# A mixture of experts whose first layer goes from split fp32r products to fp32 products on quarter tiles of TensorE

## The chip, the cores and the metric

The kernel runs on one NeuronCore of a Trainium2 chip. The metric is the time of one execution in microseconds (us), lower is better. The kernel before takes 583.3 us (median of three runs, 582.72 to 583.43).

## The reference, cut to what matters

There are 16 steps of 784 tokens, each token a vector of D = 64. Every step is embedded, runs through one step of a recurrent cell, and then through a mixture of 16 experts, of which the two with the highest logits count. The part that the change touches is the gate and the expert layers:

```python
gate_logits = x @ gate_w + gate_b                 # x: tokens x 64, gate_w: 64 x 16
topk_vals, topk_idx = jax.lax.top_k(gate_logits, 2)
topk_w = softmax(topk_vals)
h = relu(einsum('bsh,ehf->bsef', x, w1) + b1)     # w1: 16 x 64 x 128, first layer
expert_out = einsum('bsef,efh->bseh', h, w2) + b2 # w2: 16 x 128 x 64, second layer
y = x + sum(topk_w * selected expert_out)         # then a layer norm
```

The input x of this part is a layer norm of the cell's output (here x2). The recurrence makes a step wait for the one before it.

## The kernel before

All 16 experts are computed for all tokens, and the gates, zero for 14 of 16, weight the results. A step's tokens are 7 tiles of 112; in transposed form they are 784 columns, worked in two halves of 392 (HALF). Four stages of different steps run beside each other in one body of a software pipeline: embedding (step t+3), cell and norm (`mix`, t+2), gate (t+1), experts (t), and closing norm (t-1). The body goes through 16 units u, and every engine has its own in-order list of work placed at units; there is no planner. Bodies 0 to 12 hold nearly everything, bodies 13 to 15 less and less.

- **x2.** VectorE writes x2 (L481), ScalarE a copy of it rounded to fp32r (L459, `hi`), VectorE the remainder (L598, `lo`). The two stand beside each other, so one TensorE transpose per tile (`x2_turn`, L675, at u = 1) puts hi in partitions 0 to 63 and lo in 64 to 127. ScalarE copies that to xt (L384, L385, `keep_xt`).
- **Logits** (L686, u = 3): per tile one fp32r product over 128 rows, against gate weights that are split in the same way, with 32 output columns; VectorE adds the two parts and the bias (L487, L490).
- **First layer** (`first_layer`, L711), once for each expert: for each half of the columns two fp32r products with 128x128 weights (w1hi, then w1lo) into the same bank. Expert e uses pZ[e % 2] (two banks, one for each half) and waits for the ReLU of expert e-2.
- **ReLU** (L426, ScalarE), once for each expert over all 784 columns, pZ to hexp.
- **Second layer** (L724, `second_layer`, at odd u, one pair of experts late): per half two fp32 products with 128x64 weights, one on either half of the array's columns, into pO.
- **Product and sum** (VectorE L543 and L559): pO + bias, times the gates that are spread over the partitions, added up; the first sum of a step starts from xt.

ScalarE's other work stands between the ReLUs, at these units: 1 keep_xt, 2 keep_xn1t (L407, L408), 3 new_hidden (L413, L415), 5 keep_h1 (L377), 6 exp (L442), 7 a square, 8 close_center and a square (L393, L389), 9 a square, 10 the gates' copy (L447), 12 the copy of x2 (L459), 14 close_norm (L398, seven small ones). TensorE's: 1 x2_turn, 2 embed_turn (L645, waits for xt), 3 logits and recur (L653, L654, wait for keep_xn1t), 5 hidden_turn (L660) and embed_in (L635, waits for the load of xcur), 7 sum_turn (L735), 10 gates_turn (L695).

Before the first body ScalarE rounds all of w1 (L439) and GpSimd computes the remainder (L354).

Of the kernel before, what the change touches and what calls it, by code (L numbers as in the profile page):

```python
# [5 lines left out]
def vit_tower_kernel(nc, x_in, tok_w, tok_b, w_ih, w_hh, b_ih, b_hh, gate_w, gate_b,  # L6
# [18 lines left out]
    f32r = mybir.dt.float32r  # L25
# [5 lines left out]
    D = w_ih.shape[0]  # L31
# [25 lines left out]
    with ctx:  # L57
# [15 lines left out]
        w1f = sb("w1f", [2 * D, E, F])  # L73
        w1hi = sb("w1hi", [2 * D, E, F], f32r)
        w1lo = sb("w1lo", [2 * D, E, F], f32r)
        gwf = sb("gwf", [2 * D, E])
        gwhl = sb("gwhl", [2 * D, 2 * E], f32r)
# [26 lines left out]
        x2 = sb("x2", [P, TILES, D])  # L104
        x2hl = sb("x2hl", [P, TILES, 2, D], f32r)
        xt = [sb(f"xt{i}", [2 * D, TOK], f32r) for i in range(2)]
# [34 lines left out]
        MIX = Chain("mix_stage", "pre hid_odd hid hid_turned h2 square var rstd x2 hi lo "  # L141
                                 "turned_a turned_b xt_a xt_b")
        GATE = Chain("gate_stage", "logits hi_part biased max1 hit1 ranked1 first1 best1 without "
# [14 lines left out]
        gw_split = sem("gate_w_split")  # L158
        w1_split = sem("w1_split")
# [52 lines left out]
        for k in range(2):  # L212
            rows = slice(k * D, (k + 1) * D)
            cell_loads += [(cell[rows, k, :], w_ih), (cell[rows, 1 - k, :], w_hh),
                           (rbias[rows, 0:1], b_ih.unsqueeze(1)), (rbias[rows, 1:2], b_hh.unsqueeze(1)),
                           (gwf[rows, :], gate_w)]
            expert_loads += [(w1f[rows, :, :], w1)]
        cell_loads += [(gbias[:, :], gate_b.partition_broadcast(P))]
# [81 lines left out]
        def _(pool):  # L300
# [48 lines left out]
            def body(t, par, experts=False, gate=False, mix=False, embed=False, close=False):  # L349
                if close:  # L350
                    add_beta(t - 1)
                if known(t, 0) and gate:
                    pool.wait_ge(w1_split, 1)
# [18 lines left out]
        def _(act):  # L372
# [44 lines left out]

            def body(t, par, experts=False, gate=False, mix=False, embed=False, close=False):
                for u in range(E):
                    if experts:  # L420
                        n = t * E + u
                        act.wait_ge(z_ready, n + 1)
                        if not known(n, RING):

                            act.wait_ge(y_ready, t * E + 2 * (u // 2) - RING + 2)
# [11 lines left out]
                    if known(t, 0) and gate and u == 4:  # L437
                        act.wait_ge(experts_loaded, EXPERTS_LOADED)
# [26 lines left out]
            act.wait_ge(cell_loaded, CELL_LOADED)  # L465
            nc.scalar.activation(gwhl[:, 0:E], gwf[:, :], ACT.Copy).then_inc(gw_split, 1)
# [7 lines left out]
        def _(dve):  # L474
# [9 lines left out]
            def bias_logits(s):  # L484
                GATE.wait(dve, s, "logits")
                parts = pB[0:P, 0:TILES * 2 * E].rearrange("p (i k e) -> p k i e", e=E, k=2)
                nc.vector.tensor_tensor(lg[:, :, :], parts[:, 0, :, :], over_tiles(gbias[:, :], E), ALU.add)\  # L487
                    .then_inc(GATE.sem, 1)
                GATE.wait(dve, s, "hi_part")
                nc.vector.tensor_tensor(lg[:, :, :], parts[:, 1, :, :], lg[:, :, :], ALU.add).then_inc(GATE.sem, 1)  # L490
# [57 lines left out]
            def add(step, q, par):  # L548

                n = step * Q + q  # L550
                dve.wait_ge(p_ready, 2 * n + 2)
                if q == 0:

                    MIX.wait(dve, step, "xt_b")
                    sofar = xt[par][:, :].bitcast(f32)
                else:
                    dve.wait_ge(summed, n)
                    sofar = acc[par][:, :]
                nc.vector.tensor_tensor(acc[par][:, :], sofar, prod[q % RING][:, :], ALU.add).then_inc(summed, 1)  # L559

            def body(t, par, experts=False, gate=False, mix=False, embed=False, close=False):
                g, s, a, c = t + 1, t + 2, t + 3, t - 1
                for u in range(E):
# [30 lines left out]
                    if mix and u == 12:  # L594
                        norm_scale(MIX, s, 1, x2[:, :, :], h2[:, :, 0:D])
                    if mix and u == 14:
                        MIX.wait(dve, s, "hi")
                        nc.vector.tensor_tensor(x2hl[:, :, 1, :], x2[:, :, :], x2hl[:, :, 0, :].bitcast(f32),  # L598
                                                ALU.subtract).then_inc(MIX.sem, 1)
# [5 lines left out]
            dve.wait_ge(gw_split, 1)  # L605
            nc.vector.tensor_tensor(gwhl[:, E:2 * E], gwf[:, :], gwhl[:, 0:E].bitcast(f32), ALU.subtract)\
                .then_inc(gw_split, 1)
# [11 lines left out]
        def _(pe):  # L619
# [45 lines left out]
            def x2_turn(s):  # L665

                MIX.wait(pe, s, "lo")
# [5 lines left out]
                for bank, first, end in ((pA, 0, PAIRS), (pB, PAIRS, TILES)):  # L673
                    for i in range(first, end):
                        last = nc.tensor.transpose(bank[:, (i - first) * P:(i - first + 1) * P],  # L675
                                                   x2hl[:, i, :, :].bitcast(f32).rearrange("p a d -> p (a d)"),
# [3 lines left out]
            def logits(s, par):  # L680

                MIX.wait(pe, s, "xt_b")
                if known(s, 1):
                    pe.wait_ge(gw_split, 2)
# [15 lines left out]
            def first_layer(t, e, par):  # L700

                n = t * E + e
                if e == 0:
                    MIX.wait(pe, t, "xt_b")
                if known(n, 1):
                    pe.wait_ge(w1_split, 2)
                if not known(n, 2):
                    pe.wait_ge(h_ready, n - 1)
                for b in range(2):
                    for k, w in enumerate((w1hi, w1lo)):  # L710
                        last = nc.tensor.matmul(halves(pZ[e % 2])[:, b, :], w[:, e, :],  # L711
                                                xt[par][:, b * HALF:(b + 1) * HALF], start=(k == 0), stop=(k == 1))
                last.then_inc(z_ready, 1)

            def second_layer(t, q):

                n = t * Q + q
                pe.wait_ge(h_ready, 2 * n + 2)
                for b in range(2):
                    if not known(n, 1):  # L720
# [84 lines left out]
```

## Time and profile before

| | |
|---|---|
| runs | 583.43, 583.3, 582.72 us |
| the profiled execution | 584.91 us, its span 583.1 us |
| mean granted TensorE clock | 0.985 |
| TensorE busy | 534.7 us (92%) |
| VectorE busy | 430.0 us (74%) |
| ScalarE busy | 356.2 us (61%) |
| GpSimd busy | 170.2 us (29%) |
| chain that ended last | TensorE 78%: pZ L711 29%, pO L724 28% |

Busy times are sums over one profiled execution. A TensorE record is longer than the distance to the next one, since records overlap; what an instruction costs is read from start to start. The "chain that ended last" follows the execution back from its end, each time to what released the instruction.

### The profile page before, as it was taken

To read this page: it belongs to the slowest core of one execution; us is meant where nothing else is said; L and a number is where in the kernel's file an instruction comes from. 1 tells how busy PE (TensorE), PEld (TensorE's weight loads), DVE (VectorE), ACT (ScalarE), POOL (GpSimd) and SP (SyncE) were. 2 spreads that over 40 slices of the span, in tenths; PEclk is the share of its full clock that TensorE was granted. 3 is DMA by queue.
4 is the path that set the end of the run, shared out by engine and by line. 5 is a ranking of instruction groups with operands and counts; after the bars stand their busy time and mean duration, and the time that the engine had idled before them with its cause. 6 is when DMAs were issued, how large, how long until landed. Compare 5 with 4: busy or idle time off the path is not lost.

```text
span 583.1 us, 8948 instructions
## 1 busy us (share of the span) xinstructions
PE 534.7 (92%) x3138; PEld 358.0 (61%) x3138; DVE 430.0 (74%) x819; ACT 356.2 (61%) x596; POOL 170.2 (29%) x133
## 2 busy tenths in 40 slices
PE   2577999999999999999999999999999999999991
PEld 2365666576666767576666767576666657565640
DVE  1144868978787878978787888878787797886762
ACT  2236665767567674757667675757667475846561
POOL 4122011513132241513242241523232151311334
PEclk9999999999999999999999999999999899998996
DMA  3304683563819184562909174562809265462801
GB/s 79 95 15 107 146 191 75 137 145 74 194 31 233 32 181 101 125 156 63 203 22 229 46 177 105 121 161 65 203 18 219 60 142 125 107 146 71 184 0 42
DMA packets 30140, 67.45 MB, mean 116 GB/s; under 512 B 7056, under 2 KB 12432, under 8 KB 29968
## 3 DMA queue, kind: packets, MB, share of 16 engines
q1 hardware_dynamic: 30096, 66.89, 49.4%
q8 instruction: 25, 0.41, 0.3%
q14 instruction: 19, 0.16, 0.1%
HBM read 59.59 MB, written 7.28 MB: 115 GB/s over the span
## 4 chain that ended last, share of the span: by engine, by line
PE 78%; DVE 5%; ACT 5%; DMA 4%; issue 4%; POOL 2%; SPq 1%; POOLq 0%; DVEq 0%; ACTq 0%
PE pZ L711 29%; PE pO L724 28%; PE pA L660 4%; PE pA L735 4%; PE pB L635 4%; DMA xcur<-x_in 4%; ACT hexp L426 2%; PE pA L653 2%; PE pB L686 2%; PE pA L645 2%; PE pA L675 1%; DVE acc L559 1%; POOL inv_std L327 1%; SPq L293 1%; PE pB L695 1%
## 5 line engine op out<-in xcount | busy, mean ns | idle before, releaser
L426 ACT ACTIVATE hexp<-pZ,b1c 128x784 f32<-128x784 f32 x256 | 229.5, 908 | 83.1 <-PE pZ L711 80.9
L543 DVE SCALAR_TENSOR_TENSOR prod<-pO,b2c,spread 128x392 f32<-128x392 f32 x256 | 151.6, 623 | 98.4 <-PE pO L724 91.8
L724 PE MATMUL pO<-hexp,w2s 128*64 128x392 f32 x1024 | 199.8, 506 | 1.3 <-ACT hexp L426 1.3
L711 PE MATMUL pZ<-xt,w1hi 128*128 128x392 f32 x512 | 194.8, 380 | 3.7 <-ACT hexp L426 2.3
L711 PE MATMUL pZ<-xt,w1lo 128*128 128x392 f32 x512 | 175.7, 343 | 0.0
L711 PEld LDWEIGHTS pZ<-xt,w1hi 128*128 128x128 f32 x512 | 97.5, 190 | 64.1 <-issue 36.2
L327 POOL TENSOR_TENSOR inv_std<-var,nhalf 112x7 f32<-112x7 f32 x48 | 74.7, 1566 | 174.5 <-DVE var L477 174.5
L724 PEld LDWEIGHTS pO<-hexp,w2s 128*64 128x64 f32 x1024 | 70.4, 137 | 79.2 <-issue 63.9
L559 DVE TENSOR_TENSOR acc<-acc,prod 128x784 f32<-128x784 f32 x112 | 118.4, 1057 | 0.1
L711 PEld LDWEIGHTS pZ<-xt,w1lo 128*128 128x128 f32 x512 | 97.9, 191 | 0.0
L334 POOL TENSOR_TENSOR h2b<-h2c,bet 112x448 f32<-112x448 f32 x16 | 20.2, 1263 | 169.0 <-DMA h2c<-h_dram 169.0
L377 ACT ACTIVATE h<-pB 112x455 f32<-112x455 f32 x16 | 8.8, 551 | 56.2 <-PE pB L635 56.2
L477 DVE TENSOR_REDUCE var<-sq 112x7 f32<-112x455 f32 x48 | 28.6, 622 | 12.9 <-ACT sq L389 12.9
L660 PEld LDWEIGHTS pA<-half_fold,state 128*112 128x112 f32 x224 | 25.7, 193 | 13.2 <-issue 8.6
L342 POOL TENSOR_TENSOR yn<-yn,gam 112x448 f32<-112x448 f32 x16 | 18.5, 1153 | 52.1 <-ACT yn L398 52.1
L735 PEld LDWEIGHTS pA<-fold,acc 128*112 128x112 f32 x224 | 23.2, 178 | 12.6 <-issue 8.6
L660 PE MATMUL pA<-half_fold,state 128*112 128x65 f32 x224 | 28.0, 282 | 3.0 <-ACT state L415 3.0
L398 ACT ACTIVATE yn<-cen,inv_std 112x64 f32<-112x64 f32 x112 | 28.3, 336 | 2.3 <-POOL inv_std L327 2.3
L635 PE MATMUL pB<-tokw,xcur 65*112 65x65 f32 x224 | 28.7, 287 | 1.0 <-DMA xcur<-x_in 0.6
L635 PEld LDWEIGHTS pB<-tokw,xcur 65*112 65x112 f32 x224 | 27.0, 202 | 2.9 <-issue 1.4
L735 PE MATMUL pA<-fold,acc 128*112 128x64 f32 x224 | 25.4, 265 | 2.7 <-DVE acc L559 2.7
L347 POOL TENSOR_TENSOR yo<-yn,h2b 112x448 f32<-112x448 f32 x16 | 27.4, 1713 | 1.3
(74 smaller groups left out, 425.6 us busy)
## 6 DMA issues: line engine op xcount, KB each, us to landing
spread<-gates_dram SPq DMA_DIRECT2D x128, 392.0 KB, 9.0
h_dram<-h SPq DMA_DIRECT2D x16, 199.1 KB, 2.5
h2c<-h_dram SPq DMA_DIRECT2D x16, 199.1 KB, 9.7
xcur<-x_in SPq DMA_DIRECT2D x16, 196.0 KB, 9.9
out<-yo SPq DMA_DIRECT2D x16, 196.0 KB, 9.3
w1f<-w SPq DMA_DIRECT2D x2, 512.0 KB, 6.1
w2s<-w SPq DMA_DIRECT2D x1, 512.0 KB, 6.8
gates_dram<-gt SPq DMA_DIRECT2D x16, 28.0 KB, 2.0
```

Source lines behind the costliest of these rows:

```text
L327: nc.gpsimd.tensor_tensor(inv_std[:, lane, :], var[:, lane, :], nhalf[:, :], ALU.pow)\
L347: nc.gpsimd.tensor_tensor(yo[:, :, :], yn[:, :, :], h2b[:, :, :], ALU.add).then_inc(CLOSE.sem, 1)
L398: last = nc.scalar.activation(yn[:, i, :], cen[:, i, :], ACT.Copy, scale=inv_std[:, 2, i:i + 1])
L426: nc.scalar.activation(hexp[u % RING][:, :].rearrange("p (b c) -> p b c", b=2), halves(pZ[u % 2]), ACT.Relu, bias=b1c[:, u:u + 1])\
L477: nc.vector.tensor_reduce(var[:, lane, :], sq[:, lane, :, :], X, ALU.add).then_inc(chain.sem, 1)
L543: nc.vector.scalar_tensor_tensor(out=prod[q % RING][:, b * HALF:(b + 1) * HALF], in0=halves(pO)[:, b, :], scalar=b2c[:, q:q + 1], in1=spre ...
L559: nc.vector.tensor_tensor(acc[par][:, :], sofar, prod[q % RING][:, :], ALU.add).then_inc(summed, 1)
L635: last = nc.tensor.matmul(tiles_and_mean(pB)[:, i, :], xcur[:, i * P:(i + 1) * P], tokw[:, :], start=True, stop=True)
L660: last = nc.tensor.matmul(tiles_and_mean(pA)[:, i, :], state[:, i % 2, (i // 2) * P:(i // 2 + 1) * P], half_fold[:, i % 2, :], start=True, ...
L711: last = nc.tensor.matmul(halves(pZ[e % 2])[:, b, :], w[:, e, :], xt[par][:, b * HALF:(b + 1) * HALF], start=(k == 0), stop=(k == 1))
L724: last = nc.tensor.matmul(halves(pO)[k * D:(k + 1) * D, b, :], w2s[:, e, :], hexp[e % RING][:, b * HALF:(b + 1) * HALF], start=True, stop= ...
L735: last = nc.tensor.matmul(tiles_of(pA)[:, i, :], acc[par][:, i * P:(i + 1) * P], fold[:, 0:D], start=True, stop=True)
```

## The change

w1 is no longer split. It is held once, even experts in partitions 0 to 63 and odd ones in 64 to 127. x2 is written in fp32 (L481) and copied once (ScalarE, `twice`), so that after the transpose xt holds x2 in both halves of the partitions. The first layer works on a pair of experts at a time, at even u: for each half of the columns four fp32 products with 64x64 weights, for two experts (rows) and two halves of their 128 outputs (columns). Its semaphore rises once for each half, and the ReLUs come as two instructions of 392 columns, one for each expert, for one half at each unit u. The logits are fp32 products over 64 rows with 16 output columns. The first sum starts from 0.5 * xt.

```diff
-                nc.vector.tensor_tensor(lg[:, :, :], parts[:, 0, :, :], over_tiles(gbias[:, :], E), ALU.add)
-                GATE.wait(dve, s, "hi_part")
-                nc.vector.tensor_tensor(lg[:, :, :], parts[:, 1, :, :], lg[:, :, :], ALU.add).then_inc(GATE.sem, 1)
+                nc.vector.tensor_tensor(lg[:, :, :], fresh, over_tiles(gbias[:, :], E), ALU.add).then_inc(GATE.sem, 1)
...
+            def relu_half(t, q, b):
+                n = t * Q + q
+                act.wait_ge(z_ready, 2 * n + b + 1)
+                if not known(n, 2):
+                    act.wait_ge(y_ready, 2 * (n - 2) + b + 1)
+                if known(n, 1) and b == 0:
+                    act.wait_ge(experts_loaded, EXPERTS_LOADED)
+                for e in (2 * q, 2 * q + 1):
+                    nc.scalar.activation(hexp[e % RING][:, b * HALF:(b + 1) * HALF], halves(pZ[e % 2])[:, b, :],
+                                         ACT.Relu, bias=b1c[:, e:e + 1]).then_inc(h_ready, 1)
...
-                        nc.scalar.activation(hexp[u % RING][:, :].rearrange("p (b c) -> p b c", b=2),
-                                             halves(pZ[u % 2]), ACT.Relu, bias=b1c[:, u:u + 1])\
-                            .then_inc(h_ready, 1)
+                        relu_half(t, u // 2, u % 2)
...
-                        nc.scalar.activation(w1hi[:, :, :], w1f[:, :, :], ACT.Copy).then_inc(w1_split, 1)
...
-                    nc.gpsimd.tensor_tensor(w1lo[:, :, :], w1f[:, :, :], w1hi[:, :, :].bitcast(f32), ALU.subtract)\
-                        .then_inc(w1_split, 1)
...
-                        nc.scalar.activation(x2hl[:, :, 0, :], x2[:, :, :], ACT.Copy).then_inc(MIX.sem, 1)
+                        nc.scalar.activation(x2[:, :, 1, :], x2[:, :, 0, :], ACT.Copy).then_inc(MIX.sem, 1)
...
-                        nc.vector.tensor_tensor(x2hl[:, :, 1, :], x2[:, :, :], x2hl[:, :, 0, :].bitcast(f32),
-                                                ALU.subtract).then_inc(MIX.sem, 1)
...
+                    nc.vector.scalar_tensor_tensor(out=acc[par][:, :], in0=xt[par][:, :], scalar=0.5,
+                                                   in1=prod[q % RING][:, :], op0=ALU.mult, op1=ALU.add)\
+                        .then_inc(summed, 1)
...
-                    last = nc.tensor.matmul(pB[0:P, i * 2 * E:(i + 1) * 2 * E], xt[par][:, i * P:(i + 1) * P],
-                                            gwhl[:, :], start=True, stop=True)
+                    last = nc.tensor.matmul(pB[0:P, i * E:(i + 1) * E], xt[par][0:D, i * P:(i + 1) * P], gw[:, :],
+                                            start=True, stop=True)
...
-                if not known(n, 2):
-                    pe.wait_ge(h_ready, n - 1)
                 for b in range(2):
-                    for k, w in enumerate((w1hi, w1lo)):
-                        last = nc.tensor.matmul(halves(pZ[e % 2])[:, b, :], w[:, e, :],
-                                                xt[par][:, b * HALF:(b + 1) * HALF], start=(k == 0), stop=(k == 1))
-                last.then_inc(z_ready, 1)
+                    if not known(n, 1):
+                        pe.wait_ge(h_ready, 4 * (n - 1) + 2 * b + 2)
+                    for k in range(2):
+                        rows = slice(k * D, (k + 1) * D)
+                        for c in range(2):
+                            some = slice(c * D, (c + 1) * D)
+                            last = nc.tensor.matmul(halves(pZ[k])[some, b, :], w1s[rows, q, some],
+                                                    xt[par][rows, b * HALF:(b + 1) * HALF], start=True, stop=True)
+                    last.then_inc(z_ready, 1)
...
-                pe.wait_ge(h_ready, 2 * n + 2)
                 for b in range(2):
+                    pe.wait_ge(h_ready, 4 * n + 2 * b + 2)
...
-                    if experts:
-                        first_layer(t, u, par)
+                    if experts and u % 2 == 0:
+                        first_layer(t, u // 2, par)
```

## Rows read from the trace of the kernel before

**Rows 1.** Fourteen steps: stretch, length, PE, PEld, DVE, ACT, POOL busy, clock.
```profile
51.28:510.86 459.58, 452.38 (x2717) 302.08 (x2717) 368.98 (x709) 305.29 (x509) 134.43 (x92) 1.00 0.55 126
```
**Rows 2.** Groups by line and form: shapes, count | busy us, mean ns | idle before.
```profile
L724 PE MATMUL pO<-hexp,w2s 128*64 128x392 f32 x1024 | 199.8, 506 | 1.3 <-ACT hexp L426 1.3
...
L498 DVE TENSOR_TENSOR hit<-lg,tv 112x112 f32<-112x112 f32 x32 | 12.2, 380 | 1.1
...
L598 DVE TENSOR_TENSOR x2hl<-x,x2hl 112x448 fp32r<-112x448 f32 x16 | 9.9, 621 | 1.3 <-ACT x2hl L459 1.3
...
L490 DVE TENSOR_TENSOR lg<-pB,lg 112x112 f32<-112x112 f32 x16 | 4.4, 274 | 0.5
```
**Rows 3.** Timeline of TensorE, last body: start us, us, line, shapes.
```profile
542.60 0.45 PE L711 MATMUL pZ<-xt,w1hi 128*128 128x392 f32 x1
...
544.21 1.54 PE L724 MATMUL pO<-hexp,w2s 128*64 128x392 f32 x8
545.68 0.45 PE L711 MATMUL pZ<-xt,w1hi 128*128 128x392 f32 x1
```
**Rows 4.** Line 724 on TensorE in the stretch 304.72 to 305.05 us.
```profile
L724 PE MATMUL pO<-hexp,w2s x2: 543/543/543, 304.7 to 304.7; 128*64 128x392 f32 x2
```
**Rows 5.** Timeline of TensorE from expert 14 to expert 1 of the next step.
```profile
306.19 0.45 PE L711 MATMUL pZ<-xt,w1hi 128*128 128x392 f32 x1
...
308.18 1.54 PE L724 MATMUL pO<-hexp,w2s 128*64 128x392 f32 x8
309.64 0.45 PE L711 MATMUL pZ<-xt,w1hi 128*128 128x392 f32 x1
...
311.54 1.54 PE L724 MATMUL pO<-hexp,w2s 128*64 128x392 f32 x8
```
**Rows 6.** Timeline of TensorE from expert 2 to recur.
```profile
314.11 0.34 PE L711 MATMUL pZ<-xt,w1hi 128*128 128x392 f32 x1
314.29 0.34 PE L711 MATMUL pZ<-xt,w1lo 128*128 128x392 f32 x1
314.97 0.57 PE L645 MATMUL pA<-ident,xn 112*128 112x112 f32 x4 [0.34 <-ACT xt L385]
...
316.10 0.77 PE L686 MATMUL pB<-gwhl,xt 128*112 128x32 f32 x7
316.80 0.59 PE L653 MATMUL pA<-state,cell 128*64 128x448 f32 x1
```
**Rows 7.** Timeline of TensorE: hidden_turn, then embed_in.
```profile
322.11 1.59 PE L660 MATMUL pA<-half_fold,state 128*112 128x65 f32 x14
323.54 1.54 PE L635 MATMUL pB<-tokw,xcur 65*112 65x65 f32 x14
```
**Rows 8.** Timeline of ScalarE: close_center and square, copy of x2, close_norm, new_hidden.
```profile
298.36 0.54 ACT L393 ACTIVATE cen<-pA 112x448 f32<-112x448 f32 x1
...
299.41 0.90 ACT L426 ACTIVATE hexp<-pZ,b1c 128x784 f32<-128x784 f32 x1
300.21 0.57 ACT L389 ACTIVATE sq<-h 112x448 f32<-112x448 f32 x1
...
305.83 0.58 ACT L459 ACTIVATE x2hl<-x 112x448 fp32r<-112x448 f32 x1 [0.79 <-DVE x L481]
...
308.02 1.76 ACT L398 ACTIVATE yn<-cen,inv_std 112x64 f32<-112x64 f32 x7
309.69 2.88 ACT L426 ACTIVATE hexp<-pZ,b1c 128x784 f32<-128x784 f32 x3
...
317.82 0.54 ACT L413 ACTIVATE state<-pA,rb 64x336 f32<-64x336 f32 x1 [0.36 <-PE pA L654]
318.38 0.63 ACT L415 ACTIVATE state<-pA,rb 64x448 f32<-64x448 f32 x1
```
**Rows 9.** Timeline of all engines before the first expert: GpSimd's remainder, VectorE beside it.
```profile
39.88 4.51 POOL L354 TENSOR_TENSOR w1lo<-w1f,w1hi 128x2048 fp32r<-128x2048 f32 x1 [10.26 <-ACT w1hi L439]
...
41.67 2.84 DVE L498 TENSOR_TENSOR hit<-lg,tv 112x112 f32<-112x112 f32 x1
```

More of the change, by code:

```diff
@@ L24, in vit_tower_kernel @@
     f32 = mybir.dt.float32
-    f32r = mybir.dt.float32r
     i32 = mybir.dt.int32
@@ L72, in vit_tower_kernel @@
         rb = sb("rb", [2 * D, 1])
[L73 to L77, printed above, removed]
+        w1s = sb("w1s", [2 * D, Q, F])
+        gw = sb("gw", [D, E])
         b1c = sb("b1c", [F, E])
@@ L103, in vit_tower_kernel @@
         h2 = sb("h2", [P, TILES, D + 1])
-        x2 = sb("x2", [P, TILES, D])
-        x2hl = sb("x2hl", [P, TILES, 2, D], f32r)
-        xt = [sb(f"xt{i}", [2 * D, TOK], f32r) for i in range(2)]
+        x2 = sb("x2", [P, TILES, 2, D])
+        xt = [sb(f"xt{i}", [2 * D, TOK]) for i in range(2)]
         lg = sb("lg", [P, TILES, E])
@@ L140, in vit_tower_kernel @@
         EMBED = Chain("embed_stage", "h1 kept square var rstd norm turned xn1t_odd xn1t")
-        MIX = Chain("mix_stage", "pre hid_odd hid hid_turned h2 square var rstd x2 hi lo "
+        MIX = Chain("mix_stage", "pre hid_odd hid hid_turned h2 square var rstd x2 twice "
                                  "turned_a turned_b xt_a xt_b")
-        GATE = Chain("gate_stage", "logits hi_part biased max1 hit1 ranked1 first1 best1 without "
+        GATE = Chain("gate_stage", "logits biased max1 hit1 ranked1 first1 best1 without "
                                    "max2 hit2 ranked2 first2 best2 diff exp den p1 p2 g1 g2 gates turned gt")
@@ L214, in vit_tower_kernel @@
             cell_loads += [(cell[rows, k, :], w_ih), (cell[rows, 1 - k, :], w_hh),
[L215 to L218, printed above, removed]
+                           (rbias[rows, 0:1], b_ih.unsqueeze(1)), (rbias[rows, 1:2], b_hh.unsqueeze(1))]
+            expert_loads += [(w1s[rows, :, :], w1.rearrange("d (q k) f -> k d q f", k=2)[k])]
+        cell_loads += [(gw[:, :], gate_w), (gbias[:, :], gate_b.partition_broadcast(P))]
         expert_loads += [(b1c[:, :], b1), (w2s[:, :, :], w2), (b2c[:, :], b2),
@@ L351, in body @@
                     add_beta(t - 1)
-                if known(t, 0) and gate:
-                    pool.wait_ge(w1_split, 1)
-                    nc.gpsimd.tensor_tensor(w1lo[:, :, :], w1f[:, :, :], w1hi[:, :, :].bitcast(f32), ALU.subtract)\
-                        .then_inc(w1_split, 1)
                 if mix:
@@ L420, in body @@
                     if experts:
[L421 to L425, printed above, removed]
-                        nc.scalar.activation(hexp[u % RING][:, :].rearrange("p (b c) -> p b c", b=2),
-                                             halves(pZ[u % 2]), ACT.Relu, bias=b1c[:, u:u + 1])\
-                            .then_inc(h_ready, 1)
+                        relu_half(t, u // 2, u % 2)
                     if gate and u == 1:
@@ L436, in body @@
                         new_hidden(t + 2)
-                    if known(t, 0) and gate and u == 4:
-                        act.wait_ge(experts_loaded, EXPERTS_LOADED)
-                        nc.scalar.activation(w1hi[:, :, :], w1f[:, :, :], ACT.Copy).then_inc(w1_split, 1)
                     if gate and u == 6:
@@ L594, in body @@
                     if mix and u == 12:
-                        norm_scale(MIX, s, 1, x2[:, :, :], h2[:, :, 0:D])
-                    if mix and u == 14:
-                        MIX.wait(dve, s, "hi")
-                        nc.vector.tensor_tensor(x2hl[:, :, 1, :], x2[:, :, :], x2hl[:, :, 0, :].bitcast(f32),
-                                                ALU.subtract).then_inc(MIX.sem, 1)
+                        norm_scale(MIX, s, 1, x2[:, :, 0, :], h2[:, :, 0:D])
             dve.wait_ge(consts, EPS_SET)
@@ L665, in x2_turn @@
             def x2_turn(s):
-                MIX.wait(pe, s, "lo")
+                MIX.wait(pe, s, "twice")
                 if not known(s, 1):
@@ L675, in x2_turn @@
                         last = nc.tensor.transpose(bank[:, (i - first) * P:(i - first + 1) * P],
-                                                   x2hl[:, i, :, :].bitcast(f32).rearrange("p a d -> p (a d)"),
+                                                   x2[:, i, :, :].rearrange("p a d -> p (a d)"),
                                                    ident[0:P, 0:P])
@@ L698, in gates_turn, with first_layer @@
                 last.then_inc(GATE.sem, 1)
-            def first_layer(t, e, par):
-                n = t * E + e
-                if e == 0:
+            def first_layer(t, q, par):
+                n = t * Q + q
+                if q == 0:
                     MIX.wait(pe, t, "xt_b")
                 if known(n, 1):
-                    pe.wait_ge(w1_split, 2)
-                if not known(n, 2):
-                    pe.wait_ge(h_ready, n - 1)
+                    pe.wait_ge(experts_loaded, EXPERTS_LOADED)
                 for b in range(2):
-                    for k, w in enumerate((w1hi, w1lo)):
-                        last = nc.tensor.matmul(halves(pZ[e % 2])[:, b, :], w[:, e, :],
-                                                xt[par][:, b * HALF:(b + 1) * HALF], start=(k == 0), stop=(k == 1))
-                last.then_inc(z_ready, 1)
+                    if not known(n, 1):
[7 more added lines that the diff above has]
+                    last.then_inc(z_ready, 1)
             def second_layer(t, q):
                 n = t * Q + q
-                pe.wait_ge(h_ready, 2 * n + 2)
                 for b in range(2):
+                    pe.wait_ge(h_ready, 4 * n + 2 * b + 2)
                     if not known(n, 1):
```

18 lines of the change are left out of this document (3 added, 15 removed).

## The prediction

> **What bounds the kernel now.** I read the page first: TensorE is busy nearly throughout, and the chain of waits is TensorE's two expert layers. Then fourteen steps by themselves [rows 1]: 459.58 us, so 32.83 us a step, TensorE busy 452.4, VectorE 369.0, ScalarE 305.3 (66%), clock 1.00. So TensorE's own list of work sets the step, and every pause in it counts. Then the groups by form, for what each kind of work costs, and last the timelines of TensorE and ScalarE, for where TensorE pauses. I name a pair of experts q0 to q7, F its first layer and S its second.
>
> Undisturbed, F takes 1.61 us (542.60 to 544.21) and S 1.47 (544.21 to 545.68) [rows 3], a pair 3.08. Against that TensorE pauses at three places in each step:
> - F7 takes 1.99 (306.19 to 308.18) and F0 of the next step 1.90 (309.64 to 311.54) [rows 5], 0.38 and 0.29 too much. ScalarE is late: the copy of x2 at 305.83 waits for VectorE, and the ReLUs behind it wait too; then close_norm fills 308.02 to 309.69 [rows 8].
> - embed_turn waits for the copies to xt: 0.68 from the last first-layer record before it (314.29 to 314.97) where 0.18 is the usual distance (314.11 to 314.29), so 0.50 lost [rows 6].
>
> **The change part by part**, for one full step (bodies 0 to 12).
>
> 1. *The products.* S is already what F becomes: fp32 products of 392 columns in pairs of column tiles. Its first two records start together (both at 304.7) [rows 4], so tiles on different columns run at once, and eight records make 1.47 us although each lasts 506 ns [rows 2, 3]. F becomes sixteen such records. If the two row halves run beside each other as the column halves do, F also takes 1.47: 0.14 less, times 8 pairs, -1.1 us. No row here shows two row halves at once. The bounds: 1.47 if they do, some 1.31 more (eight further records at 0.33, two at a time) if not. I take the first, nearest in kind. Four tiles also need four weight loads before the first column of the last tile moves; bound for that 0 to 0.2 per F, and I take 0.03 (+0.2 a step), since part of it falls into waits that come anyway.
>
> The Trainium skill (TensorEngine Tiling (Array Packing), Key Properties) says that tiles work independently and that four 64x64 ones can run at once. By it F is 1.47 or a little more; the trace agrees for two column tiles and shows no row tiles.
>
> 2. *Logits.* Seven fp32r products in 0.70 us (316.10 to 316.80) [rows 6] become seven fp32 ones, each two records with 112 weight columns. hidden_turn is that kind: fourteen records in 1.43 us, 0.10 each [rows 7]. fp32r products with the same 112 columns also take 0.10 each, so it is the weights that count and fewer output columns help nothing. 14 x 0.10 = 1.40, so +0.7 us; bounds +0.3 (if 64 rows make a weight load cheaper) and +0.8. It is on the path: recur follows it.
>
> 3. *The wait for xt.* Between x2_turn and embed_turn stood one expert (0.8); now F1 for two experts stands there (1.47), longer than the two copies. -0.5 us. What is late next is recur, which waits for keep_xn1t: the expert that stood between is gone, but the longer logits hide it. ScalarE has the xt copies, two half ReLUs (1.0) and the two keep_xn1t copies (1.0) to do, by my count until about 3.9 us after x2_turn starts, and logits end at 0.66 + 1.47 + 0.34 + 1.4 = 3.9. So nothing left over, but nothing to spare.
>
> 4. *ScalarE.* A ReLU of 784 columns takes 0.80 from start to start (299.41 to 300.21), the seven of 64 columns 0.24 each (308.02 to 309.69) [rows 8]. The line between gives 0.49 for 392 columns; four make 1.97 us a pair where two made 1.60. The last of a row ends 0.58 after its start (between 0.54 for 336 columns and 0.63 for 448) [rows 8]. ScalarE has 4 of 32.8 us of new work, and would stay under 80% busy; the point is when. F now waits for both ReLUs of its half, and at even units ScalarE's other work stands between the first half's ReLUs and the second's. A half can be read some 0.27 after its last column (recur starts at 316.80, its 448 columns of four passes take 0.75, new_hidden starts at 317.82) [rows 6, 8]. With F4 starting at 0:
>    - F4's first half is out at 0.71, its ReLUs start at 0.98, close_center and its square follow at 1.97 and take 1.05 (298.36 to 299.41) [rows 8], the second half's ReLUs run from 3.02 to 4.1. F5 starts at 2.94 and wants them at 3.65: a pause of 0.48. Today there is none here.
>    - The x2 copy starts 2.72 after expert 12's start (305.83 against 306.19 - 3.08) [rows 3, 5, 8], as VectorE's list before it is unchanged. With F6 at 0: copy 2.72 to 3.2, ReLUs to 4.3, wanted by F7 at 3.65: 0.68 (today 0.38).
>    - Then q7's first ReLUs to 5.2, close_norm 1.67, the second ones end at 7.95. F0 of the next step starts at 6.56 and wants them at 7.27: 0.70 (today 0.29).
>
>    Together 1.86, and 0.05 each for starting again, against 0.67 today: +1.3 us.
>
> 5. *VectorE* loses the remainder of x2 (0.62) and one addition (0.27) a step [rows 2]. It is not what TensorE waits for in a full step, so 0, with +0 to -0.3 open. The first sum with a factor reads and writes the same amounts: 0 as well. The x2 copy in fp32 goes as today.
>
> 6. *Start.* The remainder of w1 on GpSimd (4.51 us) goes, and the VectorE instruction beside it took 2.84 where the mean of its kind is 0.38 [rows 2, 9]. It lies in the chain before the first expert, but the exponential behind it must also wait for a copy of h1, and the logits before it become longer at the low clock. I take -0.9, bounds -2.5 and +1.
>
> 7. *Bodies 13 to 15.* They have fewer pauses of kind 4, and pure pairs gain 0.14 each; the last ReLUs come behind close_norm as today, but half of S7 goes ahead of them. -1.5 for all.
>
> Per full step: -1.1 + 0.2 + 0.7 - 0.5 + 1.3 = +0.6, less 0.2, since slower tiles and longer waits overlap: +0.4, times 13, +5.2. With -0.9 and -1.5: +2.8. The profiled execution took 584.9 (span 583.1), so 587.7; the median lies 1.6 below it: about 586. The sum is a difference of terms larger than itself, so its sign is far from sure.
>
> The Trainium skill (TensorEngine Tiling (Array Packing), PSUM Bottleneck) warns that tiling speeds up TensorE but not the emptying of the banks, which can become the limit. That is my term 4; the trace of before shows it at two places, 0.38 and 0.29 us.
>
> **The rivals.**
> - *The pauses stay as they are today* (the half ReLUs let the next F start sooner, and the hand count above is too strict). Then a step changes by -1.1 + 0.2 + 0.7 - 0.5 = -0.7, times 14 steps and with the two last terms: -12, so 571; half of it 577. For it: ScalarE is only 66% busy. Against: today's pauses come out of the same count at the right size.
> - *Half ReLUs don't overlap.* new_hidden's two instructions, also with a bias, start 0.56 apart for 336 columns (317.82 to 318.38) [rows 8]; then 392 columns take 0.6 instead of 0.49. Each of the three places gets 0.2 to 0.4 longer and recur waits too: +1.0 a step, 600. Against: whole ReLUs do overlap.
> - *Tiles start one after another.* 0.15 more per F, half hidden in waits: +0.6 a step, 594. This decides if F measures over 1.6 us undisturbed; then the change has no gain on TensorE at all.
> - *Row halves one after the other.* F 1.31 longer: 10.5 a step, less 1.9 of pauses that vanish: 710.
>
> **How the numbers follow.** Forecast 0.45 (581 to 591), pauses as today 0.28, no overlap 0.13, slow starts 0.10, no row tiling 0.04. What this measurement can tell from no change is 0.2%, 1.2 us: faster is under 582.1. Faster takes all of the first rival and 0.05 of the forecast: 0.33. Same takes 0.16 of the forecast: 0.16. Slower is the rest, 0.51. The range from 572 to 601 leaves out the 0.04, about half a tenth below and as much above. The forecast's own range is 581 to 591.
>
> **What would show it.** TensorE's rows: F from its first record to S's first, 1.47 in the last body where nothing is late; fourteen logits records in 1.4; embed_turn directly behind F1. ScalarE's: half ReLUs 0.49 apart. F5, F7 and F0 with 0.5 to 0.7 between their halves, and none at F1 to F4. VectorE free of the 0.62. I am wrong if the sum of F's pauses per step is under 1.0 us (then it is faster) or F undisturbed is over 1.55 (then slower by more), or if the loads of xcur, which embed_in waits for, come to be what ends last.

## The result, and the profile after

| | before | changed |
|---|---|---|
| median | 583.37 us | 593.14 us |
| runs | 582.72 to 584.47 (4) | 592.04 to 594.3 (4) |
| ratio | | 1.0166, 95% interval 1.0139 to 1.0192 |
| the profiled execution | 584.91, span 583.1 | 594.3, span 591.5 |
| fourteen steps, x2_turn to x2_turn | 459.58 [rows 1] | 470.32 |

The changed kernel is slower by 9.8 us. The forecast was 586, with 572 to 601 as the range and slower as the likeliest sign: the sign was right, but the forecast change of +2.8 us is only about a quarter of what was measured, and the narrower range of 581 to 591 was missed.

The busy times of the page of the changed kernel (engine, busy us, share, instructions), and the groups that answer to L426, L711 and L686 of before:

```profile
PE 539.1 (91%) x4274; PEld 258.9 (44%) x4274; DVE 412.1 (70%) x786; ACT 392.0 (66%) x850; POOL 166.7 (28%) x132
...
L415 ACT ACTIVATE hexp<-pZ,b1c 128x392 f32<-128x392 f32 x512 | 264.9, 582 | 63.9 <-PE pZ L692 63.0
...
L692 PE MATMUL pZ<-xt,w1s 64*64 64x392 f32 x2048 | 209.6, 510 | 16.7 <-ACT hexp L415 16.7
...
L664 PE MATMUL pB<-gw,xt 64*112 64x16 f32 x224 | 26.0, 254 | 0.0
```

VectorE and GpSimd have less to do, ScalarE 36 us more, and TensorE now shows 16.7 us in which it idles before a first-layer product because a ReLU is late; before, it was 2.3 us. (Before, most of a pause was hidden in the overlap of the records; by the starts it was 0.66 us a step.) The same fourteen steps as in [rows 1], then TensorE's timeline from F6 to recur of the next step:

```profile
49.38:519.70 470.32, 455.78 (x3715) 215.23 (x3711) 357.46 (x681) 338.96 (x735) 134.72 (x92) 1.00 0.54 124
```

```profile
308.15 1.55 PE L692 MATMUL pZ<-xt,w1s 64*64 64x392 f32 x16
309.63 1.54 PE L705 MATMUL pO<-hexp,w2s 128*64 128x392 f32 x8
311.10 0.89 PE L692 MATMUL pZ<-xt,w1s 64*64 64x392 f32 x8
312.47 0.89 PE L692 MATMUL pZ<-xt,w1s 64*64 64x392 f32 x8 [0.48 <-ACT hexp L415]
313.29 1.54 PE L705 MATMUL pO<-hexp,w2s 128*64 128x392 f32 x8
314.76 0.89 PE L692 MATMUL pZ<-xt,w1s 64*64 64x392 f32 x8
316.03 0.89 PE L692 MATMUL pZ<-xt,w1s 64*64 64x392 f32 x8 [0.38 <-ACT hexp L415]
316.85 1.54 PE L705 MATMUL pO<-hexp,w2s 128*64 128x392 f32 x8
318.31 0.60 PE L655 MATMUL pA<-ident,x 112*128 112x112 f32 x4
318.75 0.45 PE L655 MATMUL pB<-ident,x 112*128 112x112 f32 x3
319.13 1.55 PE L692 MATMUL pZ<-xt,w1s 64*64 64x392 f32 x16
320.61 0.60 PE L625 MATMUL pA<-ident,xn 112*128 112x112 f32 x4
321.14 1.54 PE L664 MATMUL pB<-gw,xt 64*112 64x16 f32 x14
322.62 0.59 PE L633 MATMUL pA<-state,cell 128*64 128x448 f32 x1
```

Read the starts. A pair's first layer with nothing late is one row of sixteen records: F6 takes 308.15 to 309.63, 1.48 us. F7 is torn in two rows of eight, 311.10 to 313.29, 2.19; F0 of the next step too, 314.76 to 316.85, 2.09; F5 (not shown) takes 1.95. Behind F1 embed_turn follows without a wait (319.13 to 320.61 is 1.48 again). Logits take 321.14 to 322.62, 1.48, where they took 0.70 [rows 6]. All four tiles of a half start together, which no row of before could show:

```profile
L692 PE MATMUL pZ<-xt,w1s x4: 540/540/540, 311.1 to 311.1; 64*64 64x392 f32 x4
```

ScalarE in the same stretch, with the copy of x2 (L449) and close_norm (L386) between the two halves' ReLUs:

```profile
309.11 1.06 ACT L415 ACTIVATE hexp<-pZ,b1c 128x392 f32<-128x392 f32 x2 [0.85 <-PE pZ L692]
310.89 0.58 ACT L449 ACTIVATE x<-x 112x448 f32<-112x448 f32 x1 [0.71 <-DVE x L469]
311.37 2.00 ACT L415 ACTIVATE hexp<-pZ,b1c 128x392 f32<-128x392 f32 x4
313.25 1.77 ACT L386 ACTIVATE yn<-cen,inv_std 112x64 f32<-112x64 f32 x7
314.92 3.13 ACT L415 ACTIVATE hexp<-pZ,b1c 128x392 f32<-128x392 f32 x6
```

Four half ReLUs go from 311.37 to 313.25: 0.47 from start to start.

In full steps x2_turn comes back after 33.83 us; before it was 32.81 to 32.85, save three longer steps (33.28, 33.09 and 34.94) in which embed_in waits 0.19 to 0.50 us for xcur, the last of them with a stretch of low clock behind the wait. The difference, 1.00 us a step, is what the experiments take apart.

### The profile page after: what moved, and what is told of

Same layout as the page of the kernel before. It is cut to its first block, busy times and chain, and to the rows that moved or that the text cites. A ratio compares the mean times of both kernels' runs of the same rounds, so it can differ in the third digit from the quotient of the medians.

```text
span 591.5 us, 11566 instructions
## 1 busy us (share of the span) xinstructions
PE 539.1 (91%) x4274; PEld 258.9 (44%) x4274; DVE 412.1 (70%) x786; ACT 392.0 (66%) x850; POOL 166.7 (28%) x132
## 4 chain that ended last, share of the span: by engine, by line
PE 64%; ACT 18%; DVE 8%; issue 6%; SPq 1%; POOL 1%; DMA 1%; POOLq 0%; DVEq 0%; ACTq 0%
PE pZ L692 21%; PE pO L705 19%; ACT hexp L415 12%; PE pA L640 4%; PE pB L664 4%; PE pA L716 4%; PE pB L615 4%; ACT yn L386 4%; DVE acc L545 3%; PE pA L633 2%; DVE prod L528 2%; PE pA L625 2%; PE pA L655 2%; DVE var L465 1%; PE pB L673 1%
## 5 line engine op out<-in xcount | busy, mean ns | idle before, releaser
L415 ACT ACTIVATE hexp<-pZ,b1c 128x392 f32<-128x392 f32 x512 | 264.9, 582 | 63.9 <-PE pZ L692 63.0
L692 PE MATMUL pZ<-xt,w1s 64*64 64x392 f32 x2048 | 209.6, 510 | 16.7 <-ACT hexp L415 16.7
L692 PEld LDWEIGHTS pZ<-xt,w1s 64*64 64x64 f32 x2048 | 61.7, 132 | 132.1 <-issue 66.2
L545 DVE TENSOR_TENSOR acc<-acc,prod 128x784 f32<-128x784 f32 x112 | 116.8, 1043 | 0.1
L326 POOL TENSOR_TENSOR h2b<-h2c,bet 112x448 f32<-112x448 f32 x16 | 21.9, 1368 | 173.1 <-DMA h2c<-h_dram 173.1
L334 POOL TENSOR_TENSOR yn<-yn,gam 112x448 f32<-112x448 f32 x16 | 20.4, 1275 | 54.9 <-ACT yn L386 54.9
L640 PEld LDWEIGHTS pA<-half_fold,state 128*112 128x112 f32 x224 | 25.7, 193 | 13.2 <-issue 8.6
L386 ACT ACTIVATE yn<-cen,inv_std 112x64 f32<-112x64 f32 x112 | 28.4, 348 | 2.3 <-POOL inv_std L319 2.3
L716 PE MATMUL pA<-fold,acc 128*112 128x64 f32 x224 | 26.7, 274 | 3.2 <-DVE acc L545 3.2
L664 PE MATMUL pB<-gw,xt 64*112 64x16 f32 x224 | 26.0, 254 | 0.0
L339 POOL TENSOR_TENSOR yo<-yn,h2b 112x448 f32<-112x448 f32 x16 | 25.5, 1594 | 1.3
L664 PEld LDWEIGHTS pB<-gw,xt 64*112 64x112 f32 x224 | 24.4, 182 | 3.3 <-issue 2.7
```

What stands on the lines that cost most here:

```text
L386: last = nc.scalar.activation(yn[:, i, :], cen[:, i, :], ACT.Copy, scale=inv_std[:, 2, i:i + 1])
L415: nc.scalar.activation(hexp[e % RING][:, b * HALF:(b + 1) * HALF], halves(pZ[e % 2])[:, b, :], ACT.Relu, bias=b1c[:, e:e + 1]).then_inc(h_ ...
L545: nc.vector.tensor_tensor(acc[par][:, :], acc[par][:, :], prod[q % RING][:, :], ALU.add)\
L640: last = nc.tensor.matmul(tiles_and_mean(pA)[:, i, :], state[:, i % 2, (i // 2) * P:(i // 2 + 1) * P], half_fold[:, i % 2, :], start=True, ...
L664: last = nc.tensor.matmul(pB[0:P, i * E:(i + 1) * E], xt[par][0:D, i * P:(i + 1) * P], gw[:, :], start=True, stop=True)
L692: last = nc.tensor.matmul(halves(pZ[k])[some, b, :], w1s[rows, q, some], xt[par][rows, b * HALF:(b + 1) * HALF], start=True, stop=True)
```

## The experiments

The rival explanations for the 1.00 us a step were: **pauses** (ScalarE's place in the list makes F wait), **logits** (twice the records), **switch** (a group of full-array products beside a product on tiles costs about 0.19 us to the next start where it cost 0.03), and for the first, that the pauses would only move. Each kernel was measured beside the kernel before, whose median was 582.8 to 583.4 each time. A ratio is against the kernel before, with its 95% interval behind it.

### One part of the change alone: fp32 logits in the kernel before

```diff
-  nc.tensor.matmul(pB[0:P, i*2*E:(i+1)*2*E], xt[par][:, i*P:(i+1)*P], gwhl[:, :], ...)
+  nc.tensor.matmul(pB[0:P, i*E:(i+1)*E], xt[par][:, i*P:(i+1)*P].bitcast(f32), gwf[:, :], ...)
```

> The kernel before with one part of the change alone: logits as fp32 products (over the 128 rows of hi and lo, 16 output columns), one VectorE addition less. Theory logits: fourteen records in 1.4 us instead of seven in 0.70, all of it on TensorE's path: +0.7 us a step, 583.4 + 11 = 594. Rival (hidden): keep_xn1t or the pauses further on take it up, under +4 us.

Measured 593.69 us, ratio 1.0171 (1.0128 to 1.0213). Logits to recur went from 0.698 to 1.386 us, a step from 32.83 to 33.53. Nothing hides it. This edit by itself is as slow as the whole change, so all the other parts together come out at about nothing in the whole time. In a full step they still cost 0.30 us (33.83 against 33.53); the changed kernel wins that back ahead of the steps, where its second x2_turn comes at 49.38 us and that of this kernel at 52.61.

### The logits over 128 rows in the changed kernel

```diff
-  gw = sb("gw", [D, E])
+  gw = sb("gw", [2 * D, E])        # lower half set to zero
-  ... xt[par][0:D, i * P:(i + 1) * P], gw[:, :] ...
+  ... xt[par][:, i * P:(i + 1) * P], gw[:, :] ...
```

> The changed kernel with the logits' products over all 128 rows (the lower half of the gate weights is zero) instead of 64. Theory switch: each small group of full-array products that now stands next to products on tiles costs 0.12 to 0.16 us for the change of tiling (embed_turn to logits is 0.19 us apart where embed_turn to a full-array product was 0.03). Then that distance falls to about 0.03, the fourteen logits records still take 1.3 from first to last, and the time falls by 0.16 x 15 = 2.4 us to about 590.7. Rival (the distance comes from the weight load of a product that had to wait, whatever its rows): the distance stays 0.19 and the time 593.

Measured 591.32 us (1.0127, 1.0088 to 1.0166), a step 33.65: 0.18 less, as much as expected, but made up otherwise. Timeline of TensorE, embed_turn, logits, recur:

```profile
318.35 0.60 PE L625 MATMUL pA<-ident,xn 112*128 112x112 f32 x4
318.79 1.46 PE L664 MATMUL pB<-gw,xt 128*112 128x16 f32 x14
320.18 0.59 PE L633 MATMUL pA<-state,cell 128*64 128x448 f32 x1
```

embed_turn to logits is 0.44 instead of 0.53: the last transpose is followed after 0.10 us and not after 0.19. The other 0.09 lies between the first logits record and the second, 0.03 instead of 0.12. From the second on the records are 0.098 apart in both kernels, so 64 rows are not slower than 128. All of the 0.18 thus lies at the change of tiling, spread over two distances, and here the product is the same fp32 one on either side of the comparison. Theory switch was right, but for where it put the gain; the distance did not fall to 0.03.

### The switch by its place: gates_turn one expert later in the kernel before

```diff
-  if gate and u == 10:
+  if gate and u == 11:
       gates_turn(t + 1, embed, close)
```

> The kernel before with gates_turn behind expert 11 instead of expert 10, so that it stands between a full-array first layer and the tiled second layer. Theory switch: gates_turn to the next group grows from 0.03 to 0.19 us because that group is on tiles, while first layer to second layer (0.27) goes; about +0.07 a step, 584. Rival (0.19 belongs to the changed kernel's row tiles alone): the distance stays under 0.1.

One run, 582.12 us; its trace is what counts. Transposes of the gates (full array), now followed by the second layer (two column tiles):

```profile
301.84 0.55 PE L695 MATMUL pB<-ident,gates 112*32 112x112 f32 x4
302.32 1.54 PE L724 MATMUL pO<-hexp,w2s 128*64 128x392 f32 x8
```

From the fourth transpose's start to the second layer's is 0.189 us; in the kernel before, with a full-array first layer there, it was 0.028. No row tiles and no changed line are in this kernel, so the 0.19 does not belong to row tiles. The next product here also changes from fp32r to fp32, so by itself this run does not tell tiling from the kind of product; the logits over 128 rows do, at embed_turn. The pair and the group took 3.51 instead of 3.49, so in place of the 0.07 there is 0.02 a step; what F to S costs (0.09) is saved, as forecast.

### ScalarE's order in the changed kernel

```diff
-  if close and u == 8:          # close_center and its square
+  if close and u == 9:
-  if close and u == 14:         # close_norm
+  if close and u == 15:
-  if mix and u == 12:           # copy of x2
+  if mix and u == 13:
```

> The changed kernel, but on ScalarE close_center with its square, the copy of x2 and close_norm stand behind the second half's ReLUs of their pair (units 9, 13, 15 instead of 8, 12, 14). Theory pauses: F5, F7 and F0 lose their pauses of 0.47, 0.71 and 0.61 us, a step falls from 33.83 to about 32.05, and the time by some 25 us to 568. Rival (pauses move): ScalarE is late somewhere else, at the x2 transposes, at recur or in VectorE's list behind the square, a step stays over 33.3 and the time over 585.

Measured 601.14 us (1.0291, 1.0237 to 1.0344): slower still, full steps of 34.38 to 37.28. But not because the pauses stayed: F5, F7 and F0 all take 1.48 now. TensorE's timeline behind S1 in one of the steps:

```profile
301.44 1.59 PE L640 MATMUL pA<-half_fold,state 128*112 128x65 f32 x14
304.82 2.56 PE L615 MATMUL pB<-tokw,xcur 65*112 65x65 f32 x14 [1.79 <-DMA xcur<-x_in]
307.31 2.89 PE L692 MATMUL pZ<-xt,w1s 64*64 64x392 f32 x16
310.13 2.46 PE L705 MATMUL pO<-hexp,w2s 128*64 128x392 f32 x8
312.52 1.59 PE L716 MATMUL pA<-fold,acc 128*112 128x64 f32 x14
```

and the same stretches as windows (stretch, length, busy PE, PEld, DVE, ACT, POOL, granted clock, DMA share, GB/s):

```profile
301.44:304.82 3.38, 1.59 (x17) 1.45 (x15) 3.30 (x8) 0.03 (x1) 0.00 (x0) 1.00 0.70 168
304.82:307.31 2.49, 2.49 (x14) 2.37 (x15) 2.36 (x5) 0.00 (x0) 2.01 (x2) 0.58 0.27 82
307.31:310.13 2.82, 2.82 (x17) 0.80 (x16) 0.09 (x2) 1.71 (x4) 0.00 (x0) 0.50 0.00 0
```

embed_in waits 1.79 us for xcur. Its load stands on SyncE's queue behind the store of the closed step, which waits for close_norm, which is one pair's half later. And then the clock falls from 1.00 to 0.50, 1.2 GHz, and the next first layer takes 2.82 us instead of 1.48. The wait (0.65 to 1.95 us) and a fall of the clock come in each of the twelve full steps. In this step the pause is 1.95 us (3.38 against 1.43), and the three groups behind it take 7.70 where they take 4.41 at full clock: another 3.3. (The profiled execution is the slowest of four, 610.1 us; the others took 599 to 603, at a mean clock of 0.948 to 0.955 against 0.942.)

### The same with the load of xcur in front of the spreading and the store

```diff
-  if embed and (known(t, 0) or not known(t, 1)):
+  if embed and known(t, 0):
       load_x(t + 3)
...
   if mix:
       keep_h2(t + 2)
-  if known(t, 0) and gate:
+  if gate and embed and not (isinstance(t, int) and t + 4 >= STEPS):
       load_x(t + 4)
   if gate:
       spread_gates(t + 1, 1 - par)
   if close:
       store(t - 1)
```

(Two bodies more are written out behind the loop, so that no load goes beyond the last step.)

> The changed kernel with ScalarE's new order and with the load of the next xcur issued by SyncE right behind keep_h2 of the body before, ahead of the gates' spreading and of the store, instead of behind the store. Theory store: with the new order alone embed_in waited 1.5 to 2 us in each step for xcur, whose load stands behind the store, which stands behind close_norm; the load is now free of it, hidden_turn to embed_in is 0.10, a step is 32.05 and the time 568. Rival: the transfers of the spreading hold xcur or others up, a step stays over 33 and the time over 583.

Measured 567.48 us, ratio 0.9727 (0.9686 to 0.9768), a step 32.04.

> The same, and the logits over 128 rows. The two edits don't touch each other: the 0.18 us a step that the wider logits gave by themselves (0.09 at embed_turn, 0.09 in the records) come off again, 565.5. Rival: keep_xn1t is late for recur then and takes it up, 568.

Measured 564.92 us, ratio 0.9674 (0.9624 to 0.9724), a step 31.86. Both as expected within 0.6 us. This is the fastest kernel of the study. Its busy times, and TensorE's timeline over F0, x2_turn and F1, with no torn F in it:

```profile
PE 526.7 (93%) x4274; PEld 263.1 (47%) x4274; DVE 406.0 (72%) x786; ACT 388.9 (69%) x850; POOL 155.6 (28%) x133
```

```profile
300.63 1.55 PE L694 MATMUL pZ<-xt,w1s 64*64 64x392 f32 x16
302.11 1.54 PE L707 MATMUL pO<-hexp,w2s 128*64 128x392 f32 x8
303.58 0.60 PE L657 MATMUL pA<-ident,x 112*128 112x112 f32 x4
304.02 0.45 PE L657 MATMUL pB<-ident,x 112*128 112x112 f32 x3
304.40 1.55 PE L694 MATMUL pZ<-xt,w1s 64*64 64x392 f32 x16
```

### Was it the load's place all along?

The changed kernel with the SyncE edit alone.

> The changed kernel with the early load of xcur alone, ScalarE's order as it is. In the changed kernel hidden_turn and embed_in are 0.10 apart in every step, so xcur holds nothing up there: theory pauses expects no change, 592 to 594, and the pauses of 0.47, 0.71 and 0.61 as before. Rival (the load's place was part of the loss already): 585 or less.

Measured 593.67 us (1.0164, 1.0117 to 1.0212), a step 33.84. No part of the changed kernel's loss is the load's; it only comes to bear when the pauses are taken out.

### The same two edits in the kernel before

ScalarE's order (here x2's copy at 13 and close_norm at 15) by itself:

> The kernel before with ScalarE's copy of x2 behind the ReLU of expert 13 and close_norm behind that of expert 15 (units 13 and 15 instead of 12 and 14). Theory pauses: the pairs at expert 14 and 0 (1.98 and 1.90 us) fall to 1.61, a step from 32.83 to 32.2, the time by 9 us to 574. Rival (pauses move): no change within 2 us, since the copy of x2 or the closing norm comes later and its chain over GpSimd, the store and the load of xcur ends last.

The four runs lie apart: 575.49 and 578.12 us, and 585.08 and 586.76 at a lower mean clock (0.985 and 0.988 against 0.976 and 0.972). The ratio of the first two is 0.9884 (0.9825 to 0.9944); the median of all four, 581.6, is 1.2 us under the kernel before, so whether this edit alone gains anything is unclear, and the 574 expected was not reached. In the trace of the run of 578.12 full steps take 32.17 to 33.37. F takes 1.60 to 1.64 wherever nothing stands inside its pair, as expected, and hidden_turn to embed_in has grown from 1.51 to 1.72 us in the mean (it is 1.43 where nothing waits): the wait for xcur again, as the rival had it.

With the early load as well:

> The kernel before with ScalarE's new order and the early load of xcur. Its pauses at experts 14 and 0 are gone with the new order (pairs 1.62), and what hidden_turn waited for xcur (0.3 us a step in the mean) goes too: a step 32.15, time 573. So if the count by terms is right, the fp32 first layer is worth no more than the 0.1 us a step between the two kernels once neither of them has pauses: the 1.06 that it saves and the 0.5 of xt against 0.78 of logits and 0.7 of changes of tiling.

Measured 571.41 us, ratio 0.9801 (0.9756 to 0.9846), a step 32.17 or 32.20 in turn. So without pauses the two forms of the first layer stand at 32.18 and 32.04 a step, 571.4 and 567.5 us, and 564.9 with the wider logits: here the change is a gain, but of 0.7 to 1.1%, and 0.14 to 0.32 us a step rather than the 1.6 that F and xt promise.

### What the split of the ReLU brings: whole ReLUs in the changed kernel

```diff
-  act.wait_ge(z_ready, 2 * n + b + 1)
-  for e in (2 * q, 2 * q + 1):
-      nc.scalar.activation(hexp[e % RING][:, b * HALF:(b + 1) * HALF], halves(pZ[e % 2])[:, b, :], ...)
+  act.wait_ge(z_ready, 2 * n + 2)
+  e = 2 * q + b
+  nc.scalar.activation(hexp[e % RING][:, :].rearrange("p (b c) -> p b c", b=2), halves(pZ[e % 2]), ...)
```

(ScalarE's wait for the second layer and TensorE's waits for the ReLUs go by whole pairs too.)

> The changed kernel with whole ReLUs again, one instruction of 784 columns for each expert behind both halves of its pair (the split of the ReLU undone, the fp32 tiles kept). A pair's ReLUs would then start 1.64 after F's start and end at 3.40, while the next F starts at 2.94: 0.46 or more in every pair, and 0.6 to 1.7 more where other ScalarE work stands in it. At the three places the pause grows too. Theory: +0.5 x 5 + some 0.7 x 3 = +4.6 us a step, 593 + 65 = 658. Rival (ScalarE's saving of 0.37 us a pair makes up for it): under 600.

Measured 653.45 us (1.119, 1.1119 to 1.1262; two runs), a step mostly 37.10, but 38.7 in three, each with a stretch of low clock. Two rows of TensorE, F7 and F0 of the next step:

```profile
299.96 1.55 PE L692 MATMUL pZ<-xt,w1s 64*64 64x392 f32 x16 [0.84 <-ACT hexp L415]
...
305.10 1.55 PE L692 MATMUL pZ<-xt,w1s 64*64 64x392 f32 x16 [2.12 <-ACT hexp L415]
```

The count of starts and ends carries over roughly: 3.3 us more in most steps and 3.8 in the mean of the fourteen, against 4.6 expected (not every pair waits, since small groups stand between some). The time, 60 us more, came near the 65 expected. In this kernel a pair's ReLUs start only when both halves of F are done; the split is worth those 60 us.

### A switch less: sum_turn directly behind embed_in, in the fastest kernel

```diff
-  if close and u == 7:
+  if close and u == 5:
       sum_turn(t - 1, 1 - par, mix)
```

> The best kernel so far (new order, early x, logits over 128 rows: 564.9) with sum_turn directly behind embed_in (unit 5 instead of 7), so that the two full-array groups share one change of tiling. Theory switch: the group L718 no longer has 0.095 us before it and 0.12 behind it, -0.2 us a step, 562. Rival: h2, which VectorE writes after hidden_turn and which frees the bank, comes later than embed_in ends (by some 0.1 to 0.5 us), and nothing is won or it gets slower, 565 to 570.

Measured 589.7 us (1.0097, 1.0064 to 1.013): 25 us more than without. The rival's pause is there in each of the twelve full steps, and small; what follows it in eight of them, a fall of the clock, is not. One of the eight, in four stretches: hidden_turn and embed_in, sum_turn, the first layer, the second layer (columns as above):

```profile
290.88:294.17 3.29, 2.97 (x31) 2.86 (x29) 3.22 (x8) 0.32 (x2) 1.29 (x1) 1.00 0.29 104
294.17:295.88 1.71, 1.71 (x14) 1.59 (x14) 1.60 (x4) 0.26 (x1) 1.23 (x2) 0.84 0.44 125
295.88:298.70 2.82, 2.82 (x17) 0.80 (x16) 0.38 (x3) 1.16 (x3) 0.00 (x0) 0.50 0.32 68
298.70:300.18 1.48, 1.48 (x13) 0.49 (x9) 0.44 (x1) 1.34 (x3) 0.00 (x0) 0.98 0.00 0
```

sum_turn starts 0.49 late (the two groups before it would take 2.80 if nothing waited). In 290.88 to 295.88 TensorE does 42 small records and pauses once for 0.49 us; then the granted clock is 0.50 and the first layer takes 2.82 us. In the fastest kernel the two groups between big products take 2.90 us, and the first layer behind them is at 1.00:

```profile
312.87:315.76 2.89, 2.89 (x30) 2.82 (x28) 2.82 (x6) 0.03 (x1) 1.27 (x2) 1.00 0.23 81
315.76:317.24 1.48, 1.48 (x17) 0.52 (x17) 1.45 (x4) 1.07 (x3) 1.36 (x1) 1.00 0.00 0
```

In the other four full steps sum_turn is as late and the clock stays at 1.00, and the step takes 32.23 us:

```profile
157.10:161.88 4.78, 4.45 (x44) 4.28 (x42) 4.61 (x11) 0.58 (x2) 2.67 (x2) 1.00 0.25 83
161.88:163.36 1.48, 1.48 (x17) 0.51 (x16) 0.61 (x3) 0.51 (x2) 0.00 (x0) 1.00 0.74 83
```

So the same work with the same pause is followed by a fall in one step and not in another. Whether sum_turn there without the pause for h2 would bring a fall was not tried, and the 0.2 us a step that one change of tiling less should save can't be read from this run.

## Why the prediction was right in sign and short in size

Per full step, forecast and measured:

| term | forecast | measured |
|---|---|---|
| F in fp32 tiles, 8 pairs | -1.1 + 0.2 | -1.1 (1.478 against 1.60 to 1.64) |
| logits, twice the records | +0.7 | +0.69 |
| wait for xt | -0.5 | -0.5 |
| pauses at F5, F7, F0 | +1.3 (0.48, 0.68, 0.70 against 0.67) | +1.1 (0.47, 0.71, 0.61 against 0.66) |
| overlap of waits | -0.2 | 0 |
| changes of tiling at small groups | not in it | +0.81 (0.72 at five distances, 0.09 behind the first logits record) |
| sum | +0.4 | +1.0 |

- **Products.** Right: the two row halves run at once, and sixteen records in four tiles take what eight in two do. The allowance for a slow start of four tiles was not needed. This settles the rival "row halves one after the other", and the rival "tiles start one after another" in that form: F undisturbed is 1.48, under the 1.55 that I had named.
- **Logits.** Right in mechanism and size: fourteen fp32 records over 128 rows take 1.386 us against 0.698; one experiment has it alone at +0.70 a step and 10.9 us in all. The changed kernel's logits take 1.48; the 0.09 more is the change of tiling, not the rows.
- **Pauses.** Right at each of the three places, within 0.1 us, and taken out by moving three lines, so shown. (The prediction's own starts and ends give 0.44, 0.65 and 0.68, 0.09 less in all than the 0.48, 0.68 and 0.70 it wrote down; its +1.3 stays by rounding.) The count by starts and ends from the timeline was worth its length. The rivals "pauses as today" and "no overlap" fall: half ReLUs are 0.47 to 0.49 apart.
- **What failed** is that part 1 took F's cost as that of S and nothing beside it. What it left out is that the old first layer was a full-array one, and that every small group that leant against it did so free of a change of tiling. Five distances grew: embed_in to F and sum_turn to F from 0.07 to 0.19, x2_turn to F, embed_turn to logits and gates_turn to S from 0.03 to 0.19; together 0.72 a step. With the 0.09 behind the first logits record it is 0.81, 10.5 us in 13 steps, where the forecast was 7.1 us short. That the tiling is the cause is shown at the logits, where the same product over 128 rows takes 0.18 less; at the other four places it is inferred from the same distance of 0.19, and the next product there also went from fp32r to fp32. The rows for it stood in the trace of before: F to S and S to F each cost 0.09 more than two products of one kind, and the last logits record was followed by recur, which is on column tiles, after 0.18 us, inside the 0.70 that the prediction read as seven times 0.10.
- **Overlap.** The deduction of 0.2 had no row behind it and was wrong: the pauses and the changes of tiling lie in different places and add.
- **Luck.** That 586 is not further off is partly luck. F and the pauses came out 0.2 us a step better each than forecast (the allowances for slow starts and for starting again were not needed), which pays for half of the term left out. And the 594 of the rival "tiles start one after another" lies nearest to the measured time, although its mechanism is refuted: a time near a forecast does not prove its cause.
- **Start and end.** The first x2_turn beside the experts comes at 49.38 instead of 51.28, -1.9 where -0.9 was forecast; from the last x2_turn to the end 71.8 instead of 72.3, -0.4 where -1.5 was: two misses that cancel. The three longer steps of before, 2.8 us together, have no like in the profiled execution of the changed kernel, nor has a stretch of low clock that before has behind its last x2_turn (at 525 us); both are in the changed kernel's favour.

So +10.7 in the fourteen steps, -1.9 and -0.4: +8.4, the 8.4 between the spans.

The Trainium skill (TensorEngine Tiling (Array Packing), Key Properties) says, beside what the prediction drew on, that a change of tiling mode drains TensorE. The traces agree that such a change costs time, and give the size: 0.19 us to the next start instead of 0.03 from a full-array group to tiles, 0.18 for the same product on 64 rows instead of 128, 0.09 more between two layers. Whether what costs it is a drain, no run shows. Had I priced that sentence at the 0.09 of F to S, at each of the five places where a neighbour now changes kind, the forecast would have been 0.45 a step higher, +0.85, and the time about 592.

## What to carry to other kernels

When a group of products changes its tiling, look at its neighbours: each small full-array group that stood beside it pays from then on, and the price is in the trace where tiled and full-array work meet already. Count an in-order engine's list by starts and ends at the places where its small work stands between two halves of what another engine waits for; moving such work by one place, with one load, was worth 25.7 us here, more than twice what the change cost. And before taking out pauses ask what they hid: here a load behind a store, whose wait, with the low clock behind it, cost more than the pauses until it was moved too.

## What the runs showed of the hardware that I had not expected

- **Low clock behind small products and a pause, but not always.** With ScalarE's new order alone the granted clock falls from 1.00 to 0.50 (2.4 to 1.2 GHz) in all twelve full steps, behind hidden_turn, a pause of 0.65 to 1.95 us and some or all of embed_in. With sum_turn moved it falls in eight of twelve, with a pause of 0.49 to 0.54 us in each of the twelve. Against that, the kernel before with ScalarE's new order has a pause of 1.13 us between hidden_turn and embed_in (448.22 to 450.78) and the clock stays at 1.00. Behind hidden_turn and embed_in without a pause no trace here shows a fall in the full steps. What decides is not shown. Where it falls, a first layer takes up to 2.82 us instead of 1.48, 1.34 us more.
- **A change of tiling is paid over two distances.** Behind a full-array transpose, 64-row fp32 products start after 0.19 us and the second record 0.12 later; over 128 rows it is 0.10 and 0.03. After that both are 0.098 us apart.
- **Four tiles at once** lose nothing against two: 540 and 543 ns for the first records, and then 0.33 us from one set of tiles to the next.
